# A fused state-space, attention and expert kernel: the first batch and the first expert pass in two halves of 256 tokens

## The chip, the cores and the metric

The kernel runs on one core of one Trainium2 chip. The metric is the device time of one execution in microseconds (us). Engine names are those of the profile: PE is the matrix engine (TensorE), PEld its weight loads, DVE the VectorE, ACT the ScalarE, POOL the GpSimd, SP the SyncE, which here only issues DMAs.

## The reference, cut to what matters

For x of 8 batches x 512 tokens x 128 features, float32, four residual blocks follow each other; `ln` is a layer norm without weights.

```python
x = x + ssm(ln(x))          # per batch
x = x + ffn(ln(x))          # 8 experts, weights shared by all tokens
x = x + attention(ln(x))    # 16 heads of 8, chunked causal mask
x = x + ffn(ln(x))          # the same expert weights once more

# ssm: INNER = 64, DSTATE = 8
xb, zb = silu(conv3(h @ W_in.T))                 # two halves of 64 channels
delta  = clip(softplus(dt(xb) + b_dt), 1e-4, 1)
decay  = clip(exp(-delta * a), 1e-4, 1)
state_t = decay_t * state_{t-1} + (1 - decay_t) * tanh(b_t) * xb_t
y_t    = sum_n(state_t * tanh(c_t)) + D * xb_t   # then concat(y, zb) @ W_out.T

# ffn: H = 128, E = 8, F = 512
h = silu(x @ w_gate[e]) * (x @ w_up[e])
out = sum_e mix[:, e] * (h @ w_down[e])          # mix from two softmaxes over e
```

The state is a recurrence along the tokens of a batch, so the second half of a batch needs the state that the first half ends with.

## The kernel before, in words

The expert block is the bulk. One pass of it over a batch is called a main: `ORDER` lists 16 of them (8 batches, twice), and each has `NCH` = 32 chunks, one chunk for 128 of the 4096 expert features. Chunk c makes the gate product of its 128 features over all 512 tokens (three float32r matmuls of 512 columns, `split3`: high x high, low x high, high x low), the up product of chunk c - 1 in the same way, and the down product of chunk c - 4 (four float32 matmuls of 128 columns, which the trace lists as eight records). ACT applies silu to the gate product (L1075), DVE multiplies it by the up product (L1113), and after four chunks, one expert, DVE adds the weighed down product to the residual (L1101). Gate and up products have two PSUM banks each, so PE can run ahead of ACT and DVE by little more than a chunk.

All other work is put between the chunks by a written-out timetable. Every job (`Ssm`, `Att`, `Head`: the router and norm ahead of a main) is a generator that yields the chunk number at which its next piece is due; `interleave` merges them per engine. Each engine then executes its own list strictly in order. Slots below zero are the set-up, which has 40 steps (`SETUP`). `T_SSM[i]` holds the slots of batch i's state-space block, `T_HEAD[m]` those of main m's head.

The set-up before: SP loads x, the packed small weights and 16 raw expert weight blocks of 256 KB through the eight buffers of `h_b` (block 8 waits until block 0 has been split). ACT casts each block to its high part (L1061), POOL subtracts to get the low part (L1159). Meanwhile batch 0 goes through its state-space block. Its rates take three table loads on ACT (L463, L474, L477). Its states are formed on DVE in four steps k, one for each pair of state indices: clip the decay (L530), drive times x (L537), times B (L543), the scan along the 512 tokens (L547), times C (L553). B and C reach all partitions by matmuls into PSUM. PE adds up the output projection (L430, L443), DVE adds the residual (L594), then DVE, POOL, PE and ACT form main 0's head, and chunk 0 starts (L274). At chunk 0 PE waits for all weights to be split and loaded.

In main 0, batch 1 goes through its state-space block. There POOL does part of the four steps: clip (L630), drive times x (L632), then after DVE's scan (L584) times C (L635) and the sum over k (L639). The output projection stands at slot 23.5, the load of batch 2's x behind it on SP, and batch 2's norm on DVE at slot 24.

## Time and profile before

| what | us |
|---|---|
| median of three runs (1482.54 to 1482.89) | 1482.62 |
| the profiled execution | 1479.0 |
| its span | 1477.2 |
| PE busy in the span | 1406.2 (95%) |
| DVE busy | 962.5 (65%) |
| ACT busy | 774.5 (52%) |
| POOL busy | 577.0 (39%) |
| gate product of chunk 0 starts at | 54.59 |
| gate product of chunk 32 (main 1) starts at | 142.59 |

Times inside the kernel are from the start of the span. A matmul's modelled end overlaps the next one's start, so the distance between two starts is what one costs; busy shares of PE are upper bounds. An engine's idle time is given in brackets behind the instruction that ended it, with what released it.

### The profile page before, as it was taken

What the parts mean: (1) busy time and instruction counts of PE and PEld (TensorE: products, weight loads), DVE (VectorE), ACT (ScalarE), POOL (GpSimd) and SP (SyncE); (2) the same over time, 40 slices, a digit from 0 to 9 for tenths busy, and PEclk for the clock granted to TensorE, in tenths of its full rate; (3) what the DMA queues carried; (4) which work ended last, traced back from release to release, by engine and by line L of the source; (5) the groups of instructions that cost most, each with busy time, mean ns of one, the idle gap of its engine ahead of it and who ended that gap; (6) DMA issues with size and microseconds to landing.
All of it is one profiled execution on the core that took longest, in us unless ns stands there. A gap on an engine that the chain in (4) does not pass through costs nothing.

```text
span 1477.2 us, 27207 instructions
## 1 busy us (share of the span) xinstructions
PE 1406.2 (95%) x10580; PEld 1211.1 (82%) x10580; DVE 962.5 (65%) x2197; ACT 774.5 (52%) x1037; POOL 577.0 (39%) x513
## 2 busy tenths in 40 slices
PE   5698999999899999999999999999999999999998
PEld 3587878888788888787888878888888888888887
DVE  5656677665866667668675776757755666576543
ACT  6364738652566545646466474555644454355321
POOL 4351555533534454146531772147603531352000
PEclk9799999999999999999999999999999999999999
DMA  5120351004210420134003500062004200510000
GB/s 175 49 59 15 92 135 31 16 15 122 40 38 23 136 40 2 44 104 80 8 2 101 125 1 9 7 162 59 2 1 122 40 2 1 143 19 1 1 8 8
DMA packets 82860, 75.23 MB, mean 51 GB/s; under 512 B 5532, under 2 KB 60860, under 8 KB 82732
## 3 DMA queue, kind: packets, MB, share of 16 engines
q1 hardware_dynamic: 82732, 73.50, 19.2%
q8 instruction: 84, 1.38, 0.4%
q14 instruction: 44, 0.36, 0.1%
HBM read 60.65 MB, written 12.83 MB: 50 GB/s over the span
## 4 chain that ended last, share of the span: by engine, by line
PE 74%; DVE 10%; issue 5%; POOL 4%; ACT 4%; DMA 1%; SPq 1%; DVEq 0%; POOLq 0%; ACTq 0%
PE pd L1020 25%; PE pg L274 7%; PE pu L274 7%; PE pu L275 6%; PE pu L276 6%; PE pg L276 6%; PE pg L275 6%; PE att_ps L679 3%; DVE h L1113 2%; PE att_ps L701 1%; POOL arena L630 1%; DVE x L1101 1%; POOL arena L632 1%; DVE arena L583 1%; PE side_ps L311 1%
## 5 line engine op out<-in xcount | busy, mean ns | idle before, releaser
L1075 ACT ACTIVATE h<-pg 128x512 f32<-128x512 f32 x512 | 304.8, 599 | 637.4 <-PE pg L276 635.2
L1020 PEld LDWEIGHTS pd<-w_down,h 128*128 128x128 f32 x4096 | 510.0, 191 | 31.9 <-issue 3.5
L1020 PE MATMUL pd<-w_down,h 128*128 128x128 f32 x4096 | 524.7, 276 | 1.1 <-DVE x L1101 0.9
L1113 DVE TENSOR_TENSOR h<-h,pu 128x512 f32<-128x512 f32 x512 | 344.4, 678 | 207.9 <-PE pu L276 198.2
L274 PE MATMUL pg<-ffn_x_hi,w_gate_hi 128*128 128x512 f32 x512 | 243.8, 476 | 1.5 <-DVE ffn_x_lo L357 1.5
L274 PE MATMUL pu<-ffn_x_hi,w_up_hi 128*128 128x512 f32 x512 | 205.5, 401 | 18.0 <-DVE h L1113 17.6
L275 PE MATMUL pu<-ffn_x_lo,w_up_hi 128*128 128x512 f32 x512 | 203.2, 397 | 0.0
L276 PE MATMUL pg<-ffn_x_hi,w_gate_lo 128*128 128x512 f32 x512 | 203.0, 397 | 0.0
L275 PE MATMUL pg<-ffn_x_lo,w_gate_hi 128*128 128x512 f32 x512 | 203.0, 397 | 0.0
L276 PE MATMUL pu<-ffn_x_hi,w_up_lo 128*128 128x512 f32 x512 | 202.6, 396 | 0.0
L890 POOL TENSOR_TENSOR q_weights<-q,pack 128x512 fp32r<-128x512 f32 x136 | 142.9, 1072 | 74.0 <-DMA k<-qk_rows 74.0
L905 POOL TENSOR_TENSOR att_arena<-att_arena,r_sums 128x512 f32<-128x512 f32 (+1 forms) x72 | 73.1, 1015 | 221.4 <-DVE r_sums L780 221.4
L1101 DVE SCALAR_TENSOR_TENSOR x<-pd,mix,x 128x128 f32<-128x128 f32 x512 | 143.8, 344 | 21.0 <-PE pd L1020 15.6
L1075 ACT ACT_TABLE_LOAD x121 | 155.2, 1283 | 2.2
L274 PEld LDWEIGHTS pu<-ffn_x_hi,w_up_hi 128*128 128x128 f32 x512 | 96.3, 188 | 50.5 <-DVE h L1113 28.1
L920 POOL TENSOR_TENSOR att_arena<-att_arena 128x512 f32<-128x512 f32 (+1 forms) x72 | 72.5, 1007 | 135.7 <-DVE att_arena L771 135.6
L276 PEld LDWEIGHTS pg<-ffn_x_hi,w_gate_lo 128*128 128x128 f32 x512 | 96.7, 189 | 23.7
L276 PEld LDWEIGHTS pu<-ffn_x_hi,w_up_lo 128*128 128x128 f32 x512 | 96.5, 188 | 23.6
L275 PEld LDWEIGHTS pu<-ffn_x_lo,w_up_hi 128*128 128x128 f32 x512 | 96.5, 188 | 22.3
L274 PEld LDWEIGHTS pg<-ffn_x_hi,w_gate_hi 128*128 128x128 f32 x512 | 98.3, 192 | 9.9 <-issue 3.2
L275 PEld LDWEIGHTS pg<-ffn_x_lo,w_gate_hi 128*128 128x128 f32 x512 | 98.4, 192 | 5.0 <-issue 1.7
L630 POOL TENSOR_SCALAR arena<-arena 128x512 f32<-128x512 f32 x28 | 53.8, 1921 | 117.0 <-ACT arena L495 116.2
(190 smaller groups left out, 1555.5 us busy)
## 6 DMA issues: line engine op xcount, KB each, us to landing
arena<-bc_spread SPq DMA_DIRECT2D x56, 256.0 KB, 4.7
att_arena<-v_rows SPq DMA_DIRECT2D x64, 144.0 KB, 3.9
qk_rows<-qk_parts SPq DMA_DIRECT2D x32, 256.0 KB, 2.3
q<-qk_rows SPq DMA_DIRECT2D x32, 256.0 KB, 3.6
k<-qk_rows SPq DMA_DIRECT2D x32, 256.0 KB, 4.5
att_arena<-v_rows SPq DMA_DIRECT2D x64, 128.0 KB, 3.4
arena<-in_x SPq DMA_DIRECT2D x8, 256.0 KB, 2.9
x<-in_x SPq DMA_DIRECT2D x8, 256.0 KB, 3.4
```

Source lines behind the costliest of these rows:

```text
L274: nc.tensor.matmul(out, w[0], x_parts[0], start=first, stop=False)
L275: nc.tensor.matmul(out, w[0], x_parts[1], start=False, stop=False)
L276: return nc.tensor.matmul(out, w[1], x_parts[0], start=False, stop=last)
L630: nc.gpsimd.tensor_scalar(d, d, 1e-4, 1.0, ALU.max, ALU.min).then_inc(dec_clip, 1)
L679: last = nc.tensor.matmul(ps[:, (4 * i + g) * WK:(4 * i + g + 1) * WK], q_w[:, n % 2, i, g, :, :].rearrange("p r q -> p (r q)"), k3[:, g, ...
L890: nc.gpsimd.tensor_tensor(q_w[:, n % 2, i, :, :, :], q3[:, :, w * WQ:w * WQ + QW].bitcast(F32).unsqueeze(2) .broadcast_to([P, 4, 4, QW]), ...
L905: nc.gpsimd.tensor_tensor(u, u, rsum[:, 0:nw, :].unsqueeze(3).broadcast_to([P, nw, 4, WK]), ALU.mult).then_inc(p_norm, 1)
L920: nc.gpsimd.tensor_tensor(u, u, smax[:, 0:nw, :].unsqueeze(3).broadcast_to([P, nw, 4, WK]), ALU.subtract).then_inc(s_sub, 1)
L1020: last = nc.tensor.matmul(pd[:, t * P:(t + 1) * P], h_b[:, d % NH, t * P:(t + 1) * P], wd[:, d % NCH, :], start=d % CPE == 0 and t == 0, s ...
L1075: nc.scalar.activation(h_b[:, c % NH, :], pg[c % 2][:, :], ACT.Silu).then_inc(gate_done, 1)
L1101: nc.vector.scalar_tensor_tensor(x[:, t, :], pd[:, t * P:(t + 1) * P], mix[m % 2][:, t, e % E:e % E + 1], x[:, t, :], ALU.mult, ALU.add).t ...
L1113: nc.vector.tensor_tensor(h, h, pu[d % 2][:, :], ALU.mult).then_inc(h_done, 1)
```

## The change

Five things are changed; mains 1 to 15 and the blocks of batches 2 to 7 keep their slots.

- Batch 0's states are formed for tokens 0 to 255 in the set-up (same order of steps on DVE, 256 columns each, and the last state kept in `state_mid`), for tokens 256 to 511 in main 0 at slots 2.7, 4.7, 6.7 and 8.7 with the output projection at 9.7. B and C for the second half come by DMA (`spread_mid`) into the still unused `q3`.
- Main 0 has two heads, at slots -4.5 and 11.5. Its chunks 0 to 15 take the first 256 tokens through all 4096 features, two groups of 128 features per chunk; chunks 16 to 31 take the other 256 tokens. A chunk's PSUM tile keeps its 512 columns, and each product has six matmuls of 256 columns.
- Batch 0's first steps: the matmul for B and C ahead of the one for the rates, the low part of x ahead of the silu of z, and one table set (`natural_log_exp_and_others`) for the exponentials and the logarithm. The output transposes go ahead of the two small weight products.
- Raw weights have a buffer for each of the 16 blocks, gate and up blocks alternate, and the last eight are subtracted on POOL from slot -2 to 1. PE waits for the blocks pair by pair.
- Batch 1: its x is loaded and normalised in the set-up, its remaining slots in main 0 are moved (states from 9, 12, 15, 18 to 10.7, 13.7, 16.4, 19.1; output from 23.5 to 23.1), and the head of main 1 from 25 to 24.6. The z half of the output projection is done with 128 rows, 64 of them zero.

```diff
-T_HEAD = [-4.5, 25] + [NCH * m - 8 for m in range(2, NM)]
+
+HEADS = [(0, 0, TT // 2), (0, TT // 2, TT)] + [(m, 0, TT) for m in range(1, NM)]
+HEAD_OF = {(m, a): n for n, (m, a, _) in enumerate(HEADS)}
+T_HEAD = [-4.5, 11.5, 24.6] + [NCH * m - 8 for m in range(2, NM)]
+T_MID = dict(k=(2.7, 4.7, 6.7, 8.7), y=9.7)
...
-        return dict(ln=-33, win=-31, dt=-26, k=(-24, -23, -22, -21), y=-19)
+        return dict(st=-35, rows=-33.5, ln=-33, win=-31, dt=-26, k=(-24, -23, -22, -21), y=-19)
     if i == 1:
-        return dict(ln=1.5, win=3.5, dt=6, k=(9, 12, 15, 18), y=23.5)
+        return dict(st=-25.2, rows=-24.2, ln=-22, win=0.7, dt=7.7, k=(10.7, 13.7, 16.4, 19.1), y=23.1)
...
-        dec_0 = [dec[:, 0, :], dec[:, 1, :]] + [xb[i][:, :, :].rearrange("p t d -> p (t d)") for i in (2, 3)]
...
+        dec_0 = [pt_flat[:, 0, :], pt_flat[:, 1, :]] + [xb[i][:, :, :].rearrange("p t d -> p (t d)") for i in (2, 3)]
+        room = [att_ar[:, N_S + i * L:N_S + (i + 1) * L] for i in range(8)]
+        xb_0, zb_0, dx_0 = room[0:3]
+        bt_0 = room[3:5]
+
+        bc_mid = [[q3[:, k, i * L // 2:(i + 1) * L // 2].bitcast(F32) for k in range(KT)] for i in range(2)]
+        state_mid = sb("state_mid", [P, KT])
+
+        w_raw = [h_b[:, i, :] for i in range(NH)] + [k_room[:, g, LEFT:LEFT + L] for g in range(4)] + room[5:8] + [u_b[:, 3, :]]
...
+                    pe.wait_ge(xs_done, 1)
+                    for v in range(2):
+                        last = nc.tensor.matmul(pd[0:2 * DSTATE, :], wbc[v][:, :], xs, start=v == 0, stop=v == 1)
+                    last.then_inc(bc_raw, 1)
...
+                x_i, z_i = (xb2, zb) if i else (xb_0, zb_0)
+                nc.scalar.activation(x_i[0:INNER, :], cv[0:INNER, :], ACT.Silu).then_inc(silu_x, 1)
+                nc.scalar.activation(x_i[INNER:P, :], cv[0:INNER, :], ACT.Silu).then_inc(silu_x, 1)
+                act.wait_ge(silu_x, 2 * i + 2)
+                nc.scalar.activation(xsm, x_i, ACT.Copy, scale=pk("lo_ssm")).then_inc(xs_m, 1)
+                nc.scalar.activation(z_i[0:INNER, :], cv[INNER:P, :], ACT.Silu).then_inc(silu_z, 1)
...
-                    rates(link)
+                    act.preload_act_table_set("natural_log_exp_and_others")
                     act.wait_ge(bc_set, 1)
                     nc.scalar.copy(bc_part[0], bc_t[:, :]).then_inc(bc_hi, 1)
+                    rates(link)
                     link.wait()
...
-                    for k in range(KT):
-                        nc.scalar.activation(dec_0[k], delta, ACT.Exp, scale=neg_a[:, k:k + 1]).then_inc(dec_exp, 1)
-                    nc.scalar.activation(ctile[0], xb2, ACT.Copy, scale=pk("d_skip")).then_inc(dx_done, 1)
+                    act.wait_ge(w_small, 2)
+                    for cols, done in ((slice(0, L // 2), dec_first), (slice(L // 2, L), dec_exp)):
+                        if done is dec_exp:
+
+                            act.dma_start(bc_d[0][:, L // 2:L], bc_t[:, L // 2:L]).then_inc(mid_out, 16)
+                            nc.scalar.activation(dx_0, xb_0, ACT.Copy, scale=pk("d_skip")).then_inc(dx_done, 1)
+                            yield -21
+                        for k in range(KT):
+                            nc.scalar.activation(dec_0[k][:, cols], delta[:, cols], ACT.Exp, scale=neg_a[:, k:k + 1]).then_inc(done, 1)
...
+                    for part in range(2):
+                        if part:
+                            for k in range(KT):
+                                yield T_MID["k"][k]
+                                if k == 0:
+                                    dve.wait_ge(mid_moved, 16 * 2 * KT)
+                                d, bt = dec_0[k][:, second], bt_0[k % 2][:, second]
+                                dve.wait_ge(dec_exp, k + 1)
+                                link(nc.vector.tensor_scalar(d, d, 1e-4, 1.0, ALU.max, ALU.min))
+                                if k >= 2:
+                                    dve.wait_ge(scan_done, k - 1)
+                                link(nc.vector.scalar_tensor_tensor(bt, d, 1.0, xb_0[:, second], ALU.subtract, ALU.mult))
+                                link(nc.vector.tensor_tensor(bt, bt, bc_mid[0][k], ALU.mult))
+                                nc.vector.tensor_tensor_scan(d, d, bt, state_mid[:, k:k + 1], ALU.mult,
+                                                             ALU.add).then_inc(scan_done, 1)
+                                dve.wait_ge(scan_done, k + 1)
+                                nc.vector.tensor_tensor(d, d, bc_mid[1][k], ALU.mult).then_inc(y_done, 1)
+                        yield T_MID["y"] + 1 if part else at["y"] + 1
+                        name, cols = ("y", part - 1), (first, second)[part]
+                        b.wait(dve, name)
+                        dve.wait_ge(res_loaded[0], 16)
+                        b.free(nc.vector.tensor_tensor(x[:, cols], b.ps(name)[:, cols], x[:, cols], ALU.add), name)
+                        b.wait_free(dve, name)
+                    return
...
+        def spread_mid(sp, link, k):
+            yield -23.5
+            sp.wait_ge(mid_out, 16)
+            for k in range(KT):
+                for h in range(2):
+                    sp.dma_start(q3[h * INNER:(h + 1) * INNER, k, :].bitcast(F32).rearrange("p (s l) -> p s l", s=2),
+                                 bc_d[0][2 * k + h::DSTATE, L // 2:L].unsqueeze(0)
+                                 .broadcast_to([INNER, 2, L // 2])).then_inc(mid_moved, 16)
...
+                yield T_SSM[i]["st"] - 1 if i > 1 else -31
+
+                b.wait(sp, ("y", i - 1) if i > 1 else ("ln1", 0))
...
+                def product(out, w, c):
+                    m, f = divmod(c, NCH)
+                    x = fxh[m % 2], fxl[m % 2]
+                    if m:
+                        return split3(out[:, :], [v[:, f, :] for v in w], [a[:, :] for a in x])
+
+                    a = f // (NCH // 2) * (L // 2)
+                    for j in range(2):
+                        last = split3(out[:, j * L // 2:(j + 1) * L // 2], [v[:, 2 * (f % (NCH // 2)) + j, :] for v in w],
+                                      [v[:, a:a + L // 2] for v in x])
+                    return last
...
-                        pe.wait_ge(w_lo, 2 * E)
-                        pe.wait_ge(wd_loaded, 16 * E)
                         pe.wait_ge(pads_set, 3)
                     if c < NC:
                         m = c // NCH
-                        if c % NCH == 0:
-                            pe.wait_ge(fx_hi, m + 1)
-                            b.wait_free(pe, ("ln2", m))
+                        if (c // NCH, c % NCH) in ((0, 0), (0, NCH // 2)) or m and c % NCH == 0:
+                            n = HEAD_OF[m, TT // 2 if c == NCH // 2 else 0]
+                            pe.wait_ge(fx_hi, n + 1)
+                            b.wait_free(pe, ("ln2", n))
+                        if c < NCH // 2 and c % 2 == 0:
+                            pe.wait_ge(w_lo, c + 2)
                         if c >= 2:
                             pe.wait_ge(gate_done, c - 1)
-                        split3(pg[c % 2][:, :], [w[:, c % NCH, :] for w in wg],
-                               (fxh[m % 2][:, :], fxl[m % 2][:, :])).then_inc(g_full, 1)
+                        product(pg[c % 2], wg, c).then_inc(g_full, 1)
                     d = c - 1
                     if 0 <= d < NC:
-                        m = d // NCH
                         if d >= 2:
                             pe.wait_ge(h_done, d - 1)
-                        split3(pu[d % 2][:, :], [w[:, d % NCH, :] for w in wu],
-                               (fxh[m % 2][:, :], fxl[m % 2][:, :])).then_inc(u_full, 1)
+                        product(pu[d % 2], wu, d).then_inc(u_full, 1)
...
+                            for j in range(2):
+                                f = 2 * (d % (NCH // 2)) + j
+                                for t in range(TT // 2):
+                                    q = f // CPE % 2 * (TT // 2) + t
+                                    last = nc.tensor.matmul(pd[:, q * P:(q + 1) * P],
+                                                            h_b[:, d % NH, (2 * j + t) * P:(2 * j + t + 1) * P], wd[:, f, :],
+                                                            start=d % CPE == 0 and (j, t) == (0, 0),
+                                                            stop=d % CPE == CPE - 1 and (j, t) == (1, TT // 2 - 1))
+                            last.then_inc(down_done, 1)
+                            continue
...
+                    if c < 0 and 0 <= c + SETUP - 8 < E:
+                        split_w(c + SETUP - 8)
+
+                    if -2 <= c < 2:
+                        for j in range(2):
+                            split_w(E + 2 * (c + 2) + j)
```

Where the rows move. ACT in the set-up, from the tanh of B and C (bc_rows) to the decays; before:

```order
L468 ACTIVATE bc_rows<-pd,pack 16x512
L463 ACT_TABLE_LOAD
L463 ACTIVATE arena<-arena 128x512
L472 CAST qk_parts<-bc_rows 16x512
L474 ACT_TABLE_LOAD
L474 ACTIVATE arena<-arena 128x512
L477 ACT_TABLE_LOAD
L477 ACTIVATE arena<-arena,neg_a 128x512 x2
L477 ACTIVATE x<-arena,neg_a 128x512 x2
```

and now:

```order
L501 ACTIVATE bc_rows<-pd,pack 16x512
L503 ACT_TABLE_LOAD
L505 CAST qk_parts<-bc_rows 16x512
L496 ACTIVATE arena<-arena 128x512
L508 ACTIVATE arena<-arena 128x512
L518 ACTIVATE attn_p_t<-arena,neg_a 128x256 x2
L518 ACTIVATE x<-arena,neg_a 128x256 x2
```

One table load stands where three stood, and the decays have 256 columns (arena and attn_p_t hold decays 0 and 1, x holds 2 and 3).

DVE in main 0, around chunks 3 to 9 (h is the product of gate and up, xs_lo the input of batch 1's rates); before:

```order
L1113 TENSOR_TENSOR h<-h,pu 128x512 x2
L514 TENSOR_TENSOR xs_lo<-arena 128x512
L517 TENSOR_SCALAR arena<-side_ps,pack 128x512
L1113 TENSOR_TENSOR h<-h,pu 128x512
L524 TENSOR_SCALAR arena<-arena 128x512
L1113 TENSOR_TENSOR h<-h,pu 128x512
L1101 SCALAR_TENSOR_TENSOR x<-pd,mix,x 128x128 x4
L1113 TENSOR_TENSOR h<-h,pu 128x512 x3
L583 SCALAR_TENSOR_TENSOR arena<-arena 128x512
```

and now, ahead of the same place:

```order
L1244 TENSOR_TENSOR h<-h,pu 128x512
L554 TENSOR_TENSOR xs_lo<-arena 128x512
L1244 TENSOR_TENSOR h<-h,pu 128x512
L642 TENSOR_SCALAR attn_p_t<-attn_p_t 128x256
L645 SCALAR_TENSOR_TENSOR att_arena<-attn_p_t,att_arena 128x256
L646 TENSOR_TENSOR att_arena<-att_arena,q 128x256
L647 SCALAR_TENSOR_TENSOR attn_p_t<-attn_p_t,state_mid,att_arena 128x256
L650 TENSOR_TENSOR attn_p_t<-attn_p_t,q 128x256
L1244 TENSOR_TENSOR h<-h,pu 128x512 x2
```

Five rows of batch 0's second half (out of attn_p_t or x) stand between the products h; the same five come again for each of the four steps.

PE at the start of main 0 (L443, now L462, is batch 0's output projection, L311, now L326, the head's transposes); before:

```order
L443 MATMUL side_ps<-pack,x 128x128 x8
L311 MATMUL side_ps<-pack,ffn_rows 128x128 x4
L274 MATMUL pg<-ffn_x_hi,w_gate_hi 128x512
L275 MATMUL pg<-ffn_x_lo,w_gate_hi 128x512
L276 MATMUL pg<-ffn_x_hi,w_gate_lo 128x512
L326 MATMUL side_ps<-pack,ffn_x 128x16 x4
```

and now:

```order
L462 MATMUL side_ps<-pack,attn_p_t 128x128 x4
L462 MATMUL side_ps<-pack,x 128x128 x4
L326 MATMUL side_ps<-pack,ffn_rows 128x128 x2
L289 MATMUL pg<-ffn_x_hi,w_gate_hi 128x256
L290 MATMUL pg<-ffn_x_lo,w_gate_hi 128x256
L291 MATMUL pg<-ffn_x_hi,w_gate_lo 128x256
L289 MATMUL pg<-ffn_x_hi,w_gate_hi 128x256
```

The output projection and the transposes have half the tiles, and a gate product is twice three matmuls of 256 columns; the row of L289 at the end begins the second three.

## Rows read from the trace of the kernel before

**Rows 1.** stretch, us, busy: PE, PEld, DVE, ACT, POOL; clock, DMA

```profile
54.60:61.10 6.50, 6.50 (x22) 5.53 (x22) 2.99 (x15) 4.19 (x5) 1.26 (x2) 0.50 0.01 4
61.10:81.20 20.10, 19.12 (x103) 14.93 (x102) 11.57 (x26) 16.55 (x25) 0.00 (x0) 1.00 0.17 45
81.20:117.90 36.70, 35.13 (x216) 30.02 (x214) 21.43 (x39) 19.89 (x25) 21.79 (x15) 1.00 0.13 35
117.90:142.60 24.70, 22.08 (x134) 18.11 (x132) 14.40 (x43) 8.69 (x15) 2.52 (x4) 1.00 0.07 22
142.60:1465.50 1322.90, 1291.05 (x9991) 1118.27 (x9990) 874.80 (x1996) 698.56 (x931) 523.70 (x464) 1.00 0.19 48
```

**Rows 2.** the chain that ended last, by engine, from the page

```profile
PE 74%; DVE 10%; issue 5%; POOL 4%; ACT 4%; DMA 1%; SPq 1%; DVEq 0%; POOLq 0%; ACTq 0%
```

**Rows 3.** timeline of ACT in the set-up: start, us, engine, line, what

```profile
15.84 0.63 ACT L457 ACTIVATE arena<-arena 64x512 f32<-64x512 f32 x1
20.82 1.28 ACT L463 ACT_TABLE_LOAD   x1
23.26 1.28 ACT L474 ACT_TABLE_LOAD   x1
25.20 1.28 ACT L477 ACT_TABLE_LOAD   x1
26.50 1.34 ACT L477 ACTIVATE arena<-arena,neg_a 128x512 f32<-128x512 f32 x2
```

**Rows 4.** timeline of DVE, first and last step of batch 0, casts behind

```profile
27.25 0.43 DVE L530 TENSOR_SCALAR arena<-arena 128x512 f32<-128x512 f32 x1 [1.61 <-ACT arena L477]
45.11 0.69 DVE L553 TENSOR_TENSOR x<-x,pg 128x512 f32<-128x512 f32 x1
45.72 0.50 DVE L1121 CAST w_q_hi<-staged 128x128 fp32r<-128x128 f32 x1
```

**Rows 5.** timeline of POOL and DVE in the set-up, then DVE in main 0

```profile
31.53 14.60 POOL L1159 TENSOR_TENSOR w_up_lo<-h,w_up_hi 128x512 fp32r<-128x512 f32 x8
...
35.61 2.28 DVE L547 TENSOR_TENSOR_SCAN arena<-arena 128x512 f32<-128x512 f32 x1
...
85.89 1.22 DVE L584 TENSOR_TENSOR_SCAN arena<-arena 128x512 f32<-128x512 f32 x1
```

**Rows 6.** DVE groups by shape: count, busy us, mean ns, idle before

```profile
L1113 DVE TENSOR_TENSOR h<-h,pu 128x512 f32<-128x512 f32 x512 | 344.4, 678 | 207.9 <-PE pu L276 198.2 <-ACT h L1075 8.1
...
L763 DVE TENSOR_TENSOR att_arena<-att_ps,pack 128x512 f32<-128x512 f32 x64 | 44.0, 688 | 55.3 <-PE att_ps L679 55.1
...
L763 DVE TENSOR_TENSOR att_arena<-att_ps,pack 128x256 f32<-128x256 f32 x8 | 3.4, 420 | 0.9 <-PE att_ps L679 0.9
```

**Rows 7.** timeline, residual add on DVE, then chunk 0 on PE

```profile
47.97 0.69 DVE L594 TENSOR_TENSOR x<-side_ps,x 128x512 f32<-128x512 f32 x1 [0.24 <-PE side_ps L443]
...
54.59 0.77 PE L274 MATMUL pg<-ffn_x_hi,w_gate_hi 128*128 128x512 f32 x1 [1.49 <-DVE ffn_x_lo L357]
```

**Rows 8.** timeline of PE: neighbours with 512 columns, then with 128

```profile
62.05 0.40 PE L275 MATMUL pu<-ffn_x_lo,w_up_hi 128*128 128x512 f32 x1
62.29 0.39 PE L276 MATMUL pu<-ffn_x_hi,w_up_lo 128*128 128x512 f32 x1
...
181.19 0.28 PE L670 MATMUL att_ps<-w_v_hi,attn_x 128*128 128x128 f32 x1
181.30 0.27 PE L671 MATMUL att_ps<-w_v_lo,attn_x 128*128 128x128 f32 x1
```

**Rows 9.** timeline of ACT, POOL, PE: batch 1, first decay to last product

```profile
80.94 0.72 ACT L495 ACTIVATE arena<-arena,neg_a 128x512 f32<-128x512 f32 x1
...
112.60 1.28 POOL L639 TENSOR_TENSOR arena<-arena 128x512 f32<-128x512 f32 x1
...
115.88 1.16 PE L430 MATMUL side_ps<-pack,arena 64*128 64x128 f32 x8
```

**Rows 10.** timeline of DVE behind the load of batch 2

```profile
121.17 0.87 DVE L290 BATCH_NORM_STATS2 bn_ssm_ln<-arena 128x6 f32<-128x128 f32 x4 [4.06 <-DMA arena<-in_x]
```

300 lines of the change are left out of this document (169 added, 131 removed).

## The prediction

> **What bounds the kernel now.** I read the chain of waits first: three quarters of it is PE [rows 2], so what counts is when PE starts its 512 chunks and what each costs. Then I cut the execution at chunk starts, taken from the timeline of PE [rows 1]: chunks 0 and 1 take 6.5 us at half the granted clock (0.50), chunks 2 to 9 take 20.1 us (2.5 each), chunks 10 to 23 take 36.7 us (2.6 each), chunks 24 to 31 take 24.7 us (3.1 each), and the other 480 take 1322.9 us (2.76 each). Before 54.6 us no chunk runs. The change can win only there and lose only in the rows up to 142.6 us, since what follows keeps its order. The last stage is PE busy for 1291 of 1323 us [rows 1], so a shift of chunk 32 should arrive at the end whole. I therefore forecast the start of chunk 32, before at 142.6 us.
>
> **The set-up, step by step.** Rates. ACT does silu of z (0.63 us) ahead of the low part of x; it goes behind [rows 3]. With the transposes ahead of the small products (an estimate: 0.3 us) the rates' input is about 0.9 us earlier. Of three table loads of 1.28 us one stays [rows 3]. The second stands wholly on the path. The third starts at 25.20 beside DVE's clip of delta, 0.43 us, so some 0.8 us of it are uncovered. That is 2.1 us, and with B and C ahead of the rates and the small waits between, I get the first decay at 22.9 instead of 26.5: 3.6 us. Beside the row stands a rule: the Trainium skill (ScalarE: Activation LUTs, What ACT_TABLE_LOAD costs) puts a switch at about 2.66 us with a drain. The row at 25.20 is followed by its exponential at 26.50, so the trace has 1.30 us for the whole; by the page's figure the two loads would save some 3 us more.
>
> DVE starts the steps at 27.25 [rows 4]. Now batch 1's norm rows (four tensor_scalar, 1.1 us) stand ahead, so the start moves by 3.3 us only, to 23.9.
>
> States. Before, 27.25 to 45.80 [rows 4], 18.5 us, for 20 instructions of 512 columns. A pair of the same instruction with 512 and 256 columns takes 0.688 and 0.420 us [rows 6]: 0.27 for 256 columns and 0.15 fixed. By that the clip of 0.43 [rows 4] becomes 0.29, the three products 0.42 each. The scan takes 2.28 us in the set-up and 1.22 in main 0 [rows 5]; the set-up's stands beside POOL's unbroken 14.6 us of weight subtractions, the other in a gap of POOL's work. Now POOL does eight blocks early and has nothing to do in this stretch, so I take (1.22 - 0.15)/2 + 0.15 = 0.69. A step is 0.29 + 3 x 0.42 + 0.69 + 0.16 for the kept state = 2.40, four are 9.6; neighbours overlap by about 0.08 (45.11 + 0.69 against a next start at 45.72 [rows 4]), with 24 instructions some 1.7 us less: 7.9 us, done at 31.9. If POOL did stand beside it, a scan would be 1.2 and the sum 10.5.
>
> Tail. The casts of the attention weights (six, 45.72 to 47.73 [rows 4, 7]) hid behind PE's last products of 2.1 us; PE's part is halved now, so they come last and cost 1.75 us: residual add at 33.7 instead of 47.97 [rows 7]. From the add to chunk 0 it was 6.6 us [rows 7]; with two tiles for four the norm statistics, rows, transposes and copies lose 1.9 us: 4.7. **Chunk 0 starts at 38.4 instead of 54.6, 16.2 us earlier.** The weights don't stop it: they are loaded without waiting for a buffer, and POOL's eight late blocks (14.6 / 8 = 1.8 us each at most [rows 5]) end by 51, while chunk 8, the first that needs the ninth, comes after 60. The down weights, now behind the spread of B and C on SP, should have landed by about 40; the first down product comes after 50.
>
> **Main 0.** Chunks 0 and 1 again cost about 6.5 us at the low clock, and batch 1's first matmuls come into them: chunk 2 at 45.2 against 61.0, 15.8 us earlier.
>
> Matmuls. Three of 512 columns become six of 256, for gate and for up. Neighbours start 0.235 us apart with 512 columns and 0.11 apart with 128 [rows 8]. No row has 256. A line between them gives 0.153, the 128-column row 0.11. I take 0.13, near half of 0.235, because at 512 columns the weight load lies hidden behind the stream. Twelve at 0.13 are 1.56 against 6 x 0.235 = 1.41, so +0.15 a chunk, +4.8 us in 32 chunks; the ends are -3 and +13.8 us. The Trainium skill (TensorE: Matmul & The Clock Gate, Back-to-back issue gap) has a sustained 81 ns at 128 columns and 131 ns at 512. Both are below this case's 110 and 235, so the measurement decides; by the page twelve matmuls would cost 1.2 to 1.3 us and main 0 would win 3 to 6 us instead of losing 5.
>
> VectorE. Four steps of 2.4 us come into slots 2.7 to 9.7. In these seven chunks it also has nine products h (0.68, about 0.61 apart [rows 6]) 5.5 us, one weighing 1.1, batch 1's input, rates and clip 1.9: 18.1 us, where PE needs 7 x 2.4 + 1.0 = 17.8. It is full there, and PE waits an estimated 1.3 us. The second half's output projection is 24 records of PE, 2.4 us. Against that batch 1's input product and transposes are already done (1.7 us). Chunk 10 at 68.2 against 81.2: **13.0 earlier**.
>
> From there batch 1 sets the pace. Before, from its first decay to POOL's last sum it is 80.94 to 113.88, 32.9 us, of which POOL works or waits for the scan in a chain; PE took the result at 115.88, two microseconds late [rows 9]. Now the first decay's slot is 1.7 later (near 73.3), the chain ends at about 105.8, and slot 23.1 comes before that, so PE waits for it: PE leaves the projection at 106.9 against 117.9, **11 earlier**. In chunks 10 to 23 the dearer matmuls are therefore mostly hidden by this chain.
>
> Chunks 24 to 31 pay their 0.15 each, 1.2 us. The wait of DVE for batch 2's x (4.06 us [rows 10]) stays. **Chunk 32 comes 10 us earlier.** In batches 2 to 7 the low part of x is 0.63 us earlier as well; DVE has work there, so I count nothing, at most 1 us of gain.
>
> The profiled execution took 1479.0 us (span 1477.2), 3.6 below the median of 1482.6. So 1479.0 - 10 = 1469.0, and on the scale of the median 1472.6 us.
>
> **The rivals.**
>
> 1. The gain is largely handed back in main 0. The matmul stands near the line (0.15), of which chunks 0 to 9 and 24 to 31 pay 0.4 each (18 x 0.25 = 4.5 more than I took), and full DVE costs 2 us more. 10 - 6.5 = 3.5: 1479.1. For it: DVE has no slack there by my sum. Against it: PEld is below PE in every stage [rows 1].
>
> 2. Slower: a 256-column matmul isn't cheaper by enough. Outside the matmuls the change is worth 10 + 3 (what I charged in chunks 0 to 9 and 24 to 31) = 13 us; if all 32 chunks paid, the point of no gain is 13 / (32 x 12) = 0.034 above half of 0.235, so about 0.152. At 0.17, 12 x 0.17 - 1.41 = 0.63 a chunk, 20 us: 7 slower, 1489.6. For it: a quarter of the columns costs not a quarter but nearly half [rows 8]. Against it: it lies above the line between two measured sizes.
>
> 3. The start is not what is waited for: batch 1's chain or batch 2's load ends at its old time, and chunk 32 comes as before, 1482. For it: chunks 10 to 31 hold idle time on PE. Against it: each link is issued in program order, so it starts when its slot does; nothing in it hangs on absolute time.
>
> 4. More is won: chunks at 0.11 to 0.12 and no wait for DVE, 16 us in all: 1466.6. The page's matmul rule would end here.
>
> **How the numbers follow.** Forecast 0.60 (gain 6 to 14: 1468.6 to 1476.6), rival 1 0.20 (half of it beyond 3 us), rival 2 0.08, rival 3 0.04, rival 4 0.08. A measurement of this kernel tells 0.2%, 3.0 us, from no change. Faster: 0.60 + 0.08 + 0.11 = 0.79. Same: 0.09 + 0.03 = 0.12. Slower: 0.09. The range goes from rival 4, somewhat beyond, to just under no change: 1464 to 1482, which leaves out rival 2 and some of each side.
>
> **What would show it.** First gate matmul at 37 to 40 us; one table load between the tanh and the first decay; scans of 256 columns at 0.7 us in the set-up; the six matmuls 0.12 to 0.14 us apart once the clock is up; DVE busy over nine tenths in the twenty microseconds behind chunk 2; PE idle in front of batch 1's output projection; main 1 on starting near 132.6 and the rest 1323 us as before. A start that isn't 14 us earlier, a spacing over 0.15, or a rest that differs by more than 3 us would make the forecast wrong.

## The result and the profile after

The changed kernel takes 1470.94 us (median of 4 runs, 1469.75 to 1472.17), the kernel before 1482.76 us in the same series. The ratio is 0.9919, with a 95% interval of 0.9902 to 0.9936: about 12 us faster. 1472.6 us had been predicted. A second series on another chip gave 0.9916 (0.9904 to 0.9928).

The profiled execution took 1470.57 us (span 1468.7). Cut nearly as [rows 1] was, the columns being stretch, length, busy time of PE, PEld, DVE, ACT and POOL, granted clock, DMA:

```profile
39.77:46.40 6.63, 6.63 (x25) 5.60 (x26) 1.07 (x3) 4.82 (x8) 5.62 (x5) 0.50 0.02 6
46.40:67.09 20.69, 17.89 (x149) 16.88 (x148) 18.98 (x44) 12.01 (x18) 0.00 (x0) 1.00 0.01 2
67.09:108.23 41.14, 37.82 (x330) 37.27 (x328) 27.09 (x58) 23.58 (x32) 22.73 (x17) 1.00 0.20 52
108.23:132.80 24.57, 22.08 (x182) 20.74 (x180) 14.98 (x44) 8.61 (x15) 2.55 (x4) 1.00 0.08 23
132.80:1455.70 1322.90, 1291.78 (x9987) 1120.88 (x9986) 874.35 (x1995) 698.04 (x930) 524.75 (x464) 0.99 0.19 48
```

The first cut here is the end of the stretch at half clock (46.40), not the start of chunk 2 (45.52); the other cuts are the starts of chunks 0, 10, 24 and 32, and the last stretch was given the length that it has in [rows 1]. Chunk 0 starts 14.8 us earlier than before, chunk 10 14.1, chunk 24 9.7, chunk 32 9.8. So 5.0 of the 14.8 us are lost inside main 0, nearly all of it between chunks 10 and 24, where 36.7 us became 41.1. TensorE's idle time accounts for 1.8 of these 4.5 us (3.3 us for 1.6); the rest is work (see whole_states). DVE is nearly full behind the first cut, 18.98 of 20.69 us; in [rows 1] it had 11.57 of 20.10.

The set-up of the profile after answers to [rows 3], [rows 4] and [rows 7]. Columns: start, duration, engine, line, operation, and in brackets the idle time before it:

```profile
18.94 1.28 ACT L503 ACT_TABLE_LOAD   x1
22.54 0.51 ACT L518 ACTIVATE attn_p_t<-arena,neg_a 128x256 f32<-128x256 f32 x1 [0.49 <-DVE arena L564]
23.94 0.49 DVE L572 TENSOR_SCALAR attn_p_t<-attn_p_t 128x256 f32<-128x256 f32 x2
25.55 0.68 DVE L592 TENSOR_TENSOR_SCAN attn_p_t<-attn_p_t,att_arena 128x256 f32<-128x256 f32 x1
31.61 0.22 DVE L1252 CAST w_q_hi<-staged 128x128 fp32r<-128x128 f32 x1
33.25 0.42 DVE L655 TENSOR_TENSOR x<-side_ps,x 128x256 f32<-128x256 f32 x1
35.56 1.26 POOL L1292 TENSOR_TENSOR w_gate_lo<-k_room,w_gate_hi 128x512 fp32r<-128x512 f32 x1
35.62 2.50 DVE L312 TENSOR_SCALAR ffn_rows<-x,mv_ffn_ln,rstd_ffn_ln 128x128 f32<-128x128 f32 x2 [1.15 <-POOL rstd_ffn_ln L320]
36.77 1.26 POOL L1292 TENSOR_TENSOR w_up_lo<-k_room,w_up_hi 128x512 fp32r<-128x512 f32 x1
39.77 0.55 PE L289 MATMUL pg<-ffn_x_hi,w_gate_hi 128*128 128x256 f32 x1 [1.12 <-DVE ffn_x_lo L374]
```

One table load is left ahead of the first decay, the states of the first 256 tokens take 7.7 us (23.94 to 31.69) where those of all 512 took 18.5, and a scan of half the length takes 0.68 us. The add is at 33.25 us. Then comes what the prediction did not have: the two normalised row tiles take 2.50 us. The same pair takes 0.6 us elsewhere (below). POOL begins its eight late weight subtractions 0.06 us before them.

In main 0, the matmuls of 256 columns, and TensorE's waits:

```profile
47.03 0.28 PE L289 MATMUL pu<-ffn_x_hi,w_up_hi 128*128 128x256 f32 x1
47.15 0.28 PE L290 MATMUL pu<-ffn_x_lo,w_up_hi 128*128 128x256 f32 x1
47.26 0.28 PE L291 MATMUL pu<-ffn_x_hi,w_up_lo 128*128 128x256 f32 x1
...
50.58 0.39 PE L289 MATMUL pu<-ffn_x_hi,w_up_hi 128*128 128x256 f32 x1 [0.67 <-DVE h L1244]
53.55 0.38 PE L289 MATMUL pu<-ffn_x_hi,w_up_hi 128*128 128x256 f32 x1 [1.28 <-DVE h L1244]
...
97.07 0.39 PE L289 MATMUL pu<-ffn_x_hi,w_up_hi 128*128 128x256 f32 x1 [1.54 <-DVE h L1244]
107.31 1.16 PE L475 MATMUL side_ps<-pack,arena 128*128 128x128 f32 x8 [1.61 <-POOL arena L720]
```

Neighbours are 0.11 to 0.12 us apart (0.114 in the median of main 0), nearly half of the 0.235 of [rows 8]; the prediction took 0.13. The last row is batch 1's output projection, which waits for POOL; it answers to the last of [rows 9], 115.88 us.

### The profile page after: what moved, and what is told of

Same layout as the page of the kernel before. It is cut to its first block, busy times and chain, and to the rows that moved or that the text cites. A ratio compares the mean times of both kernels' runs of the same rounds, so it can differ in the third digit from the quotient of the medians.

```text
span 1468.7 us, 27670 instructions
## 1 busy us (share of the span) xinstructions
PE 1401.1 (95%) x10772; PEld 1220.7 (83%) x10772; DVE 968.2 (66%) x2232; ACT 772.3 (53%) x1043; POOL 575.4 (39%) x517
## 4 chain that ended last, share of the span: by engine, by line
PE 75%; DVE 10%; issue 5%; POOL 4%; ACT 3%; DMA 0%; DVEq 0%; POOLq 0%; ACTq 0%
PE pd L1135 25%; PE pg L289 7%; PE pu L289 7%; PE pu L290 6%; PE pu L291 6%; PE pg L291 6%; PE pg L290 6%; PE att_ps L760 3%; DVE h L1244 2%; POOL arena L711 2%; PE att_ps L782 1%; DVE x L1232 1%; POOL arena L713 1%; DVE arena L664 1%; DVE ffn_rows L312 1%
## 5 line engine op out<-in xcount | busy, mean ns | idle before, releaser
L1135 PEld LDWEIGHTS pd<-w_down,h 128*128 128x128 f32 x3840 | 480.3, 192 | 30.1 <-issue 3.6
L1135 PE MATMUL pd<-w_down,h 128*128 128x128 f32 x3840 | 494.6, 277 | 1.2 <-DVE x L1232 1.1
L289 PE MATMUL pg<-ffn_x_hi,w_gate_hi 128*128 128x512 f32 (+1 forms) x544 | 249.7, 459 | 1.1 <-DVE ffn_x_lo L374 1.1
L289 PE MATMUL pu<-ffn_x_hi,w_up_hi 128*128 128x512 f32 (+1 forms) x544 | 210.8, 388 | 19.7 <-DVE h L1244 19.5
L290 PE MATMUL pu<-ffn_x_lo,w_up_hi 128*128 128x512 f32 (+1 forms) x544 | 208.6, 383 | 0.0
L291 PE MATMUL pg<-ffn_x_hi,w_gate_lo 128*128 128x512 f32 (+1 forms) x544 | 208.6, 383 | 0.0
L290 PE MATMUL pg<-ffn_x_lo,w_gate_hi 128*128 128x512 f32 (+1 forms) x544 | 208.5, 383 | 0.0
L291 PE MATMUL pu<-ffn_x_hi,w_up_lo 128*128 128x512 f32 (+1 forms) x544 | 208.2, 383 | 0.0
L1232 DVE SCALAR_TENSOR_TENSOR x<-pd,mix,x 128x128 f32<-128x128 f32 x480 | 134.7, 343 | 21.0 <-PE pd L1135 15.9
L289 PEld LDWEIGHTS pu<-ffn_x_hi,w_up_hi 128*128 128x128 f32 x544 | 102.6, 189 | 50.1 <-DVE h L1244 28.9
L289 PEld LDWEIGHTS pg<-ffn_x_hi,w_gate_hi 128*128 128x128 f32 x544 | 104.9, 193 | 9.2 <-issue 2.8
```

The costliest lines, as they stand in the source:

```text
L289: nc.tensor.matmul(out, w[0], x_parts[0], start=first, stop=False)
L290: nc.tensor.matmul(out, w[0], x_parts[1], start=False, stop=False)
L291: return nc.tensor.matmul(out, w[1], x_parts[0], start=False, stop=last)
L1135: last = nc.tensor.matmul(pd[:, t * P:(t + 1) * P], h_b[:, d % NH, t * P:(t + 1) * P], wd[:, d % NCH, :], start=d % CPE == 0 and t == 0, s ...
L1232: nc.vector.scalar_tensor_tensor(x[:, t, :], pd[:, t * P:(t + 1) * P], mix[m % 2][:, t, e % E:e % E + 1], x[:, t, :], ALU.mult, ALU.add).t ...
```

## The experiments

Each kernel was timed in rounds with the kernel before; ratios are to that. The runs down to halves_all are of one chip, those from after_again on of another, where the changed kernel itself took 1469.08 us: its own variants there are to be held against that. "First chunk" is the first gate matmul in the trace; it, chunk 32 and the span are of one profiled execution each. That of chain_piped was the fastest of its six (1467.68 us), 4.8 us under their median.

| kernel | median us | ratio (95%) | first chunk | chunk 32 | span |
|---|---|---|---|---|---|
| rows_first | 1468.60 | 0.9915 (0.9900 to 0.9929) | 37.93 | 131.09 | 1466.8 |
| tables_back | 1472.47 | 0.9940 (0.9927 to 0.9953) | 41.49 | 133.44 | 1469.9 |
| whole_states | 1477.24 | 0.9973 (0.9962 to 0.9984) | 51.03 | 138.90 | 1474.7 |
| halves_all | 1461.57 | 0.9872 (0.9853 to 0.9891) | 39.72 | 131.83 | 1458.8 |
| after_again | 1469.08 | 0.9916 (0.9904 to 0.9928) | 39.93 | 131.89 | 1466.0 |
| casts_later | 1476.03 | 0.9958 (0.9944 to 0.9972) | 45.80 | 138.73 | 1474.5 |
| chain_piped | 1472.48 | 0.9935 (0.9920 to 0.9949) | 39.69 | 134.93 | 1465.9 |
| all_four | 1468.62 | 0.9912 (0.9900 to 0.9923) | 42.23 | 137.13 | 1466.1 |
| slots_early | 1472.18 | 0.9933 (0.9920 to 0.9945) | 40.19 | 133.71 | 1470.7 |
| rows_halves | 1459.93 | 0.9846 (0.9833 to 0.9860) | 38.03 | 130.08 | 1458.2 |
| before_halves | 1475.61 | 0.9956 (0.9943 to 0.9968) | 55.14 | 143.74 | 1475.7 |
| best | 1462.52 | 0.9862 (0.9846 to 0.9879) | 38.46 | 132.99 | 1461.9 |

**rows_first.** Why did the rows take 2.50 us?

```diff
                     if -2 <= c < 2:
+                        if c == -2:
+                            pool.wait_ge(ln_sems["ffn_ln"][2], TT // 2)
                         for j in range(2):
```

> GpSimd starts its eight late weight subtractions only when VectorE has written head 0's two normalised row tiles; nothing else differs from the changed kernel (1470.9 us, first chunk at 39.8 us of the trace). Theory A (the 1.2 us that the two tiles took each, beside 0.3 us elsewhere, is GpSimd working at the same time, and the first chunk waits for them): the pair takes 0.6 us, the first chunk starts at 37.9 us, and since nothing before chunk 32 waits for anything but TensorE's and batch 1's chain, which start from there, the whole is 1.0 to 1.9 us shorter, 1469.0 to 1469.9 us. Rival B (the pair is slow for itself, its operands or a wait that the row hides): the pair stays at 2.5 us and nothing moves. Rival C (the start is not what the middle of main 0 waits for): first chunk 1.9 us earlier, chunk 32 and the end where they were.

```profile
35.66 0.60 DVE L312 TENSOR_SCALAR ffn_rows<-x,mv_ffn_ln,rstd_ffn_ln 128x128 f32<-128x128 f32 x2 [1.15 <-POOL rstd_ffn_ln L320]
36.34 1.26 POOL L1292 TENSOR_TENSOR w_gate_lo<-k_room,w_gate_hi 128x512 fp32r<-128x512 f32 x1 [0.72 <-DVE ffn_rows L312]
37.93 0.55 PE L289 MATMUL pg<-ffn_x_hi,w_gate_hi 128*128 128x256 f32 x1 [1.12 <-DVE ffn_x_lo L374]
```

The pair takes 0.60 us, the first chunk comes 1.84 us earlier, and from the add (33.29) to it are 4.6 us. Theory A holds, and rivals B and C are out: chunk 32 is 1.7 us and the span 1.9 us shorter than in the profile after, which had stretches of low clock of the same lengths. The ratio, 0.9915, can't tell 1.9 us apart from the changed kernel's 0.9916; the traces do.

**casts_later.** The six casts behind the rows instead of ahead of the add.

```diff
-                    yield T_SSM[0]["y"] + 0.5
+                    yield -2.5
                     both([w[:, :] for w in wq], pk("w_q"))
```

> VectorE's six casts of the attention weights (1.7 us together) move from ahead of the residual add in the set-up to behind head 0's normalised rows. Theory A (the prediction's: the add had been ready before the casts ended, their 1.7 us stood bare on the way to the first chunk): the add starts at 31.7 to 32.0 us instead of 33.25, the first chunk at 38.2 to 38.6 us instead of 39.8, and the whole is 1.2 to 1.6 us shorter, about 1469.5 us. Rival B (TensorE's last output matmul, not the casts, releases the add, or the casts delay the low part of head 0's rows by as much): first chunk and end within 0.4 us of the changed kernel.

Both theories fell: its first chunk and chunk 32 come 6.0 and 5.9 us later than in the changed kernel, and its median is 7.0 us above after_again's. VectorE's timeline:

```profile
35.24 2.50 DVE L312 TENSOR_SCALAR ffn_rows<-x,mv_ffn_ln,rstd_ffn_ln 128x128 f32<-128x128 f32 x2 [1.15 <-POOL rstd_ffn_ln L320]
37.66 1.30 DVE L1252 CAST w_q_hi<-staged 128x128 fp32r<-128x128 f32 x1
38.98 1.25 DVE L1253 TENSOR_TENSOR w_q_lo<-staged,w_q_hi 128x128 fp32r<-128x128 f32 x1
...
43.96 1.25 DVE L1281 TENSOR_TENSOR w_v_lo<-staged,w_v_hi 128x128 fp32r<-128x128 f32 x1
45.13 0.41 DVE L374 TENSOR_TENSOR ffn_x_lo<-side_ps,ffn_x_hi 128x256 fp32r<-128x256 f32 x1
```

Each cast, 0.22 to 0.29 us at 31.61 in the changed kernel, now takes as long as one of POOL's subtractions (1.26 us), and the low half of head 0's rows waits behind all six. So casts and rows are slow for the same reason. The instruction with one operand in PSUM, at 45.13, keeps its time. The add itself came only 0.4 us earlier (32.86): with the casts away TensorE releases it. From the end of the last state product to the add it is 0.80 us here and 1.56 in the changed kernel, so 0.8 us of the casts stood bare, not 1.75.

**tables_back.** The exponential ahead of the rounding again, no named set.

```diff
-                    act.preload_act_table_set("natural_log_exp_and_others")
+                    rates(link)
                     act.wait_ge(bc_set, 1)
                     nc.scalar.copy(bc_part[0], bc_t[:, :]).then_inc(bc_hi, 1)
-                    rates(link)
```

> The changed kernel with the table order of the kernel before in the set-up: softplus' first exponential ahead of the rounding of the B and C rows, no named table set, so two more table loads. Theory A (set-up time passes one to one to the end): with two loads more of 1.28 us each and the copy behind the exponential, the first decay moves from 22.5 us to 25.1 or 26.0 us, the first chunk from 39.8 to 42.4 to 43.3 us and the end by the same 2.6 to 3.5 us: 1473.5 to 1474.4 us. Rival C (main 0 is bound by batch 1's chain or by VectorE and swallows part of the start): the first chunk moves as much, the end by under 1 us.

```profile
18.82 1.28 ACT L496 ACT_TABLE_LOAD   x1
...
21.27 1.28 ACT L507 ACT_TABLE_LOAD   x1
...
23.21 1.28 ACT L517 ACT_TABLE_LOAD   x1
24.51 0.51 ACT L517 ACTIVATE attn_p_t<-arena,neg_a 128x256 f32<-128x256 f32 x1
```

The first decay is 2.0 us later, for two loads that make 2.6: the last of them runs while VectorE's clip is awaited, of which the changed kernel has 0.49 us left as idle time (its row at 22.54). The profiles of after and of after_again differ in main 0 by the length of the low clock, 6.6 and 3.7 us of it; here it was 3.8, so after_again is the one to compare with. Against it the first chunk is 1.6 us later and chunk 32 is 1.6 us later: what the start loses reaches chunk 32 one to one. Rival C is out. Theory A is right in kind, but its 2.6 to 3.5 us were too much: it had not taken off the wait for the clip.

**whole_states.** The second half's states in the set-up too.

```diff
-T_MID = dict(k=(2.7, 4.7, 6.7, 8.7), y=9.7)
+T_MID = dict(k=(-17.8, -17.8, -17.8, -17.8), y=-17)
```

> The changed kernel with the states of batch 0's second 256 tokens also in the set-up, right behind those of the first, instead of between chunks 2 and 9 of main 0; the halves of main 0's products stay. Theory A (moving this half beside main 0's matmuls is where the gain is from): four steps of 2.4 us on VectorE and the second half's output rows stand ahead of the first chunk, which starts at about 50 us; VectorE is then free in chunks 2 to 10, where TensorE waited about 3 us in all, so that chunk 32 comes 7 us later than in the changed kernel and the whole takes about 1478 us. Rival B (the window in which VectorE is full costs about as much as the move gives): the whole is within 3 us of the changed kernel, under 1474 us.

```profile
51.03:75.77 24.74, 23.35 (x173) 22.05 (x173) 11.50 (x27) 16.78 (x25) 5.63 (x5) 0.91 0.01 3
75.77:114.20 38.43, 35.10 (x306) 34.55 (x304) 26.60 (x57) 23.57 (x32) 22.71 (x17) 1.00 0.21 56
114.20:138.90 24.70, 21.96 (x182) 20.64 (x180) 14.98 (x44) 8.62 (x15) 2.55 (x4) 1.00 0.08 23
```

The first chunk is 11.3 us later, chunk 32 only 6.1, and the whole takes 1477.24 us. Theory A had 50 us, 7 us and about 1478 us and holds; rival B, under 1474 us, is out. Main 0 takes 87.9 us here, 93.0 in the changed kernel, 88.0 before. The 5.2 us between the first two are: chunks 0 to 10 2.6 us (1.4 of waits, since of the changed kernel's 0.67 and 1.28 us only one of 0.54 is left; 1.0 of clock, 4.6 us at the low level for 6.6), and chunks 10 to 24 2.7 us. The latter is no wait: TensorE is idle for 3.3 us in this stretch in both. It is TensorE's second output projection of batch 0, in the changed kernel:

```profile
68.55 0.60 PE L455 MATMUL side_ps<-pack,att_arena 128*128 128x128 f32 x4
68.99 0.61 PE L462 MATMUL side_ps<-pack,att_arena 128*128 128x128 f32 x4
69.44 1.06 PE L462 MATMUL side_ps<-pack,attn_p_t 128*128 128x128 f32 x8
70.33 1.06 PE L462 MATMUL side_ps<-pack,x 128*128 128x128 f32 x8
```

These 24 records take 2.7 us (68.55 to 71.22), and in the set-up most of them lie beside VectorE's steps. So of the 11.3 us that hiding the second half wins at the start about 5 are paid back, and it is still worth 6.1. The other 3.6 us of the earlier first chunk (54.59 to 51.03) come from the rest of the change.

**chain_piped.** GpSimd's order for batch 1, k and k+1 interleaved, with closer slots:

```diff
+                    steps = [(0, 0), (1, 0), (0, 1), (2, 0), (1, 1), (3, 0), (2, 1), (3, 1)]
-k=(10.7, 13.7, 16.4, 19.1), y=23.1)
+k=(10.7, 12.4, 15.6, 18.4), y=23.1)
+T_SSM[1].update(bc=[8.7, 10.4, 14.4, 16.6], ct=[14.0, 17.2, 20.0, 21.9], tot=15.1)
```

> Batch 1's state steps in main 0: GpSimd clips the decays of step k+1 and multiplies its drive before it multiplies step k's states with C, instead of after; the slots of batch 1's steps are closer by 0.7 to 1.3 chunks. Work and its amount are the same. Theory A (from chunk 16 to 24 main 0 waits for GpSimd's chain of 8.1 us a step, which stands still 2.1 to 3.8 us in each step while VectorE scans, and this is where 5.0 of the 14.8 us won at the first chunk were given back): a step takes about 6 us, the chain ends near 100 us instead of 107.3, TensorE's waits of 1.5 us at 95.5 and 1.6 us at 105.7 go, chunk 32 starts about 3 us earlier and the whole is near 1468 us. Rival B (VectorE is the bound there): the waits turn up elsewhere and the whole is within 0.8 us of the changed kernel.

```profile
88.37 0.38 PE L292 MATMUL pu<-ffn_x_hi,w_up_hi 128*128 128x256 f32 x1 [2.35 <-DVE h L1252]
89.50 3.20 PE L1135 MATMUL pd<-w_down,h 128*128 128x128 f32 x16 [0.16 <-DVE x L1234]
106.94 0.38 PE L292 MATMUL pu<-ffn_x_hi,w_up_hi 128*128 128x256 f32 x1 [1.58 <-DVE h L1252]
```

Rival B's mechanism is what happened, the waits turn up elsewhere, but the loss is past its 0.8 us: the median is 3.4 us above after_again's. Chunk 32 comes 2.1 us later than in the profile after, 1.4 of it by 2.9 us more at the low clock. VectorE stands idle for 2.50 us until GpSimd's product at 85.12, and the products h queue behind it; where the engines now do overlap, two of its four scans take 2.18 us for 1.22.

**slots_early.** Only the slots, near those before.

```diff
-k=(10.7, 13.7, 16.4, 19.1), y=23.1)
+k=(9.7, 12.7, 15.4, 18.1), y=23.1)
```

> The changed kernel with batch 1's four state steps one chunk earlier in main 0 (slots 9.7, 12.7, 15.4, 18.1 for 10.7, 13.7, 16.4, 19.1; the kernel before had 9, 12, 15, 18). Theory A (chunks 20 to 24 wait for these steps, and it is the change's later slots that make them late against the chunks: 1.5 us of TensorE at 95.5 us and 1.6 us at 105.7 us, for 0.6 and 1.0 us in the kernel before): the first decay runs at about 72.7 us instead of 74.9, the chain ends 2.2 us earlier at 105 us, the second wait goes and chunk 24 starts 1 to 1.6 us earlier, whole 1467.5 to 1468.5 us. Rival B (what is earlier for batch 1 is later for the hidden products on VectorE): waits of the same size elsewhere, whole within 0.5 us of the changed kernel.

The chain did end 2.9 us earlier (104.36) and the wait at batch 1's projection is gone. But TensorE waits 3.21 us from 94.13 on where it waited 1.54. VectorE then:

```profile
93.46 1.18 DVE L388 TENSOR_TENSOR mix_sums<-mix_sums 128x2 f32<-128x2 f32 x1
94.56 0.16 DVE L389 TENSOR_REDUCE mix_sums<-mix 128x2 f32<-128x16 f32 x1
94.75 1.23 DVE L390 SCALAR_TENSOR_TENSOR mix_sums<-mix_sums 128x2 f32<-128x2 f32 x1
```

Head 1's routing, instructions on two numbers a partition, 0.16 and 0.38 us in the changed kernel, fell beside two of GpSimd's (93.34 and 94.70 us) and the product h stood behind them. This is rival B's mechanism, two waits of 1.54 and 1.61 us exchanged for one of 3.21, but not its size: the median is 3.1 us above after_again's. In main 0 what is lost beyond the waits is clock: the granted clock falls at 97.04 us, 0.3 us before the long wait ends.

```profile
97.34 0.58 PE L289 MATMUL pu<-ffn_x_hi,w_up_hi 128*128 128x256 f32 x1 [3.21 <-DVE h L1244]
```

and the stretch that follows (columns as in the first view above, granted clock third from the end):

```profile
97.10:100.40 3.30, 3.06 (x14) 3.06 (x15) 3.11 (x8) 0.12 (x2) 2.15 (x2) 0.50 0.00 0
```

The changed kernel has full clock in this place (its row from 67.09 to 108.23 says 1.00). chain_piped fell too, at 90.1, 1.7 us behind its wait of 2.35 us. From chunk 10 to chunk 24 it took 41.9 us here for 41.1, with TensorE idle for 3.2 us in place of 3.3. The half clock can be at most 1.7 us of it, so the chain that ended 2.9 us earlier was worth 0.9 us at chunk 24 at most.

**halves_all, before_halves, rows_halves.** Halves of 256 columns in every main.

```diff
                     if m:
-                        return split3(out[:, :], [v[:, f, :] for v in w], [a[:, :] for a in x])
+                        for j in range(2):
+                            s = slice(j * L // 2, (j + 1) * L // 2)
+                            last = split3(out[:, s], [v[:, f, :] for v in w], [v[:, s] for v in x])
+                        return last
```

> The changed kernel with every gate and up product of mains 1 to 15 also issued as two halves of 256 columns (480 chunks, 12 matmuls of 256 columns for 6 of 512 in each), the same weights read twice. In the prediction a chunk of halves was taken to cost 0.15 us more. Theory A (a 256-column matmul follows its like every 0.1155 us as main 0 shows, half of the 0.2348 us of 512 columns): six extra weight loads are hidden and the whole is within 0.3% of 1470.9 us, 1466 to 1475 us, rather shorter. Rival B (the term of the prediction, 0.13 us apart): 480 times 0.15, 72 us longer, about 1543 us. Rival C (the pitch at the first rows' fall of speed, 0.153 us): about 1680 us.

> The kernel before, with nothing of the change but this: every gate and up product issued as two halves of 256 columns, in all 512 chunks. Theory A (256 columns take 0.114 to 0.1155 us from start to start, 512 take 0.2345 us: 0.018 us less a chunk at least): 9 us or more shorter, 1470 to 1473 us for 1481 us. Rival B (in the changed kernel the halves help for another reason, its shorter main 0): within 3 us of the kernel before. Rival C (0.15 us more a chunk, as the prediction's term had it): 1558 us.

> The changed kernel with the late weight subtractions behind head 0's rows and with halves of 256 columns in all mains. If the two effects add (first chunk 1.9 us earlier; 480 chunks at 0.02 us): 1460 us, first chunk at 37.9 us. If the gain of the halves is only that fewer stretches at the lower granted clock fell into its runs: 1465 us or more.

Halves are not dearer but a little cheaper. halves_all takes 1461.57 us, below even theory A's 1466 to 1475; its rivals B and C are out, and rows_halves met its sum of 1460 us. From chunk 32 to the end, halves_all and rows_halves take 1326.9 and 1328.1 us; the changed kernel and its variants with the same later code and 17.1 us at the low clock take 1334.1 to 1336.9 (after_again, slots_early); halves_all had 10.2 us of it there and rows_halves 13.7. The cleanest figure is that of mains 12, 13 and 14, which have full clock in every profile: 85.51, 85.09 and 85.55 us with 512 columns, both in the kernel before and in the changed one, and 84.9, 84.6 and 85.0 us with halves, in before_halves too. That is 0.5 to 0.6 us a main, 0.015 to 0.018 us a chunk. In the kernel before, the same edit and nothing else gives 0.9956, 6.7 us (4.7 to 8.4), with main 0 no shorter. Of its medians that is 0.013 us a chunk: theory A had the sign and, at full clock, nearly the 0.018 us, but 9 us or more was too much for the whole; rivals B and C of before_halves are out (B's bound was 3 us). Part of the 7.6 us between rows_halves and rows_first is clock: 13.7 us at the low level behind chunk 32 for 17.1, half of the difference being 1.7. Which part of issuing halves saves the time was not tried. rows_halves is the fastest kernel of the study: 22 us under the kernel before, 9 to 11 under the changed one.

**all_four and best.** Combinations: rows_first, casts_later, chain_piped and halves_all in the first; rows_first, halves_all, slots_early and the casts between statistics and rows (slot -4.2) in the second.

> The changed kernel with four edits at once: late weight subtractions behind head 0's rows, the casts behind these rows, batch 1's steps interleaved on GpSimd, and halves of 256 columns in every main. If their effects add (1.9, 1.4, 3 and 10 us): 1454.5 us. If the clock's later stretches differ or the chain's gain fails: 1457 to 1460 us.

> The changed kernel with four edits: late weight subtractions behind head 0's rows; halves of 256 columns in all mains; batch 1's steps one chunk earlier; VectorE's six casts between head 0's statistics and its rows, where VectorE waits 1.1 us for GpSimd's root and GpSimd's subtractions have not begun. If the casts keep 0.25 to 0.3 us each, the residual add comes 1.0 us earlier (TensorE's last output matmul then releases it) and the rows 0.4 us earlier or not at all. Sum of the four: 1.9, 9, 1.5 and 0.4 us, 1456 to 1458 us. If the slots bring nothing: 1459 us.

Both missed their forecasts, all_four (1468.62 us) by 8 us or more and best (1462.52 us) by 3.5. all_four's casts took 1.17 to 1.32 us except the first, and its chain was chain_piped's: two losses that I had counted as gains. In best the casts keep their 0.19 to 0.29 us, GpSimd being held back, but nothing is won by it: the add came at 33.43 because TensorE's last matmul came late, and the casts then delay the rows by 0.4 us. It is 2.6 us behind rows_halves: the wait of 3.21 us of slots_early is in it (it ends at 95.39 us), and from 94.7 on 6.8 us at half clock, worth up to 3.4.

**after_again** was the control on the chip of the second series.

> The changed kernel itself once more, on the same chip as the three that follow: every theory expects 1470.9 us within 0.15% and the granted clock at its lower level from 36 to 46 us; the spread of its runs tells how much of a difference between kernels is the number of later stretches at the lower level.

1469.08 us is inside the band; the low clock in it ended at 43.6 us, not 46.

## Why the prediction was right, and which steps were wrong

The sum came out within 1.7 us of the measured median, and chunk 32, on which it rested, at 132.80 for 132.6. The mechanism was right: the first chunk starts earlier by the states and the table loads taken off its way, main 0 hands part of it back, and the rest passes through. That it fits to 0.2 us is luck. By stretches the errors are +1.4 us up to chunk 0, -2.5 from there to chunk 10, +2.4 to chunk 24 and -1.1 to chunk 32. Point by point:

- **First decay 22.9, step start 23.9, states done 31.9:** 22.54, 23.94 and 31.69. Right, the scan of 0.69 (0.68) and the overlap of neighbours with it. tables_back shows the tables' share, 2.0 us.
- **Casts 1.75 us bare, add at 33.7:** add at 33.25. The casts hide between TensorE's products to all but some 0.8 us (casts_later, all_four: 0.80 us from the last state product to the add, for 1.56).
- **Add to chunk 0 in 4.7 us, chunk 0 at 38.4:** failed, 6.5 us and 39.77. The step scaled the old tail by the number of tiles and asked only whether GpSimd's late subtractions would be there in time for chunk 8, not what they do to VectorE beside them. rows_first shows 1.84 us for it, and 4.6 us from the add to chunk 0 without them. The row was there to see in the scan of 2.28 us [rows 5], which I had used for the states alone. The Trainium skill has the mechanism (SBUF — State Buffer, SBUF: two separate sides): VectorE and GpSimd share a pair of ports that one of them holds for its whole instruction. By that rule each of two row tiles would wait out one subtraction of 1.26 us, 2.5 us together. The trace agrees: 2.50 us.
- **Chunk 0 to chunk 10 in 29.8 us:** 27.3. Two terms were wrong. The dearer matmul, 0.13 us for 0.114: I took 0.15 us a chunk for it, 1.2 to 1.5 us here. And the second output projection, booked at 2.4 us in this stretch, stands at 68.55 us, behind chunk 10, as slot 9.7 and its waits would have told. Full DVE was right: 1.95 us of waits for an estimated 1.3.
- **From there batch 1 sets the pace, chunk 24 at 106.9:** failed in part, 108.23. TensorE does wait at the projection, 1.61 us where it waited for nothing before, and the first decay was at 74.94 for 73.3, the chain's end at 107.26 for 105.8. But of the 4.5 us that this stretch grew by, the waits are 1.8 and the second output projection 2.7, and in slots_early, whose chain ends 2.9 us earlier, TensorE is idle in this stretch for as long as ever (3.2 us for 3.3): it waits for VectorE's queue instead.
- **Chunks 24 to 31 1.2 us longer:** 24.57 for 24.71, no longer. This is the dearer matmul again.
- **The rest as before, 1323 us:** 1335.9 us from chunk 32 to the span's end for 1334.6. Within 3 us, but not by staying equal. At full clock in both profiles mains 1, 5, 9 and 11 are 0.4 to 0.5 us shorter than before (95.07 to 94.61 us for main 1) and mains 2, 4, 8 and 12 to 15 equal; this gain, 1.6 us in these four, was put at nothing, "at most 1 us". No run isolates it. More time at half clock takes it back and more, see below.

Some sums of the prediction don't come out as written. Its terms for chunk 10 give 12.6 us earlier, not 13.0, and the states with POOL beside them take 10.0 us by its terms, not 10.5. The line between the two sizes of [rows 8] gives 0.152 us at 256 columns, which is the very point of no gain of rival 2, so that rival's "against it" was worth nothing. What speaks against it is the measurement: 256 columns take nearly what 128 take (0.11) and half of what 512 take (0.235). The three sizes fit a spacing with a floor near 0.11 that is proportional above it; no other size was tried.

Rival 4 had the matmuls right (0.11 to 0.12) but not the waits. Rival 1, part of the gain handed back in main 0, is what happened in kind (5.0 of 14.8 us), and the forecast held that part in it. Rival 3 is out by tables_back and rows_first.

## What to carry to other kernels

A long element-wise block that is put on GpSimd "where it has nothing to do" cost each of the casts, row scalings and two-operand instructions that VectorE did beside it on SBUF alone about one whole GpSimd instruction, so look at what VectorE does on the critical path in that window and hold the block back by one semaphore. When half of a serial phase is hidden behind a busy engine, charge the hiding: here it gave back about 5 us of 11, half of it not as waits but as TensorE's own work that had been nearly free in the set-up. Splitting a 512-column product into two of 256 cost nothing here even though the weights are loaded twice.
